# Attention and output projection one head later, V projected in a unit's third step, one DMA transpose for both halves of a head's result

## The reference

```python
q, k, v = h @ dequant(q_w), h @ dequant(k_w), h @ dequant(v_w)   # 32, 8, 8 heads of 128
q, k = rope(q), rope(k)
k, v = repeat(k, 4), repeat(v, 4)
scores = einsum('bhqd,bhkd->bhqk', q, k) * 128 ** -0.5 + mask    # causal
attn = softmax(scores)
out = einsum('bhqk,bhkd->bhqd', attn, v)
y = out.reshape(b, s, 4096) @ dequant(o_w)                       # 4096 -> 512
```

## Time and profile before

| what | us |
|---|---|
| median of 3 runs (lowest, highest) | 1589.76 (1585.22, 1591.85) |
| the profiled execution: its own time, its span | 1594.79, 1593.0 |
| busy in the span: PE, DVE, ACT, POOL | 1440.8, 1218.2, 936.1, 914.7 |
| granted PE clock, mean | 0.978 |

### The profile page before, as it was taken

One profiled execution on the slowest core, in us unless ns is written; L12 is line 12 of the kernel. 1 busy time (PEld: TensorE's weight loads), 2 busy tenths in 40 slices (PEclk: granted clock), 3 DMA queues, 4 the chain that ended last, 5 costly groups with the idle time before them and its releaser, 6 DMA issues.

```text
span 1593.0 us, 41176 instructions
## 1 busy us (share of the span) xinstructions
PE 1440.8 (90%) x11104; PEld 858.2 (54%) x11104; DVE 1218.2 (76%) x2884; ACT 936.1 (59%) x2198; POOL 914.7 (57%) x642
## 2 busy tenths in 40 slices
PE   5787898999999999998999999988999986999998
PEld 3454555556555555655555555555555553544543
DVE  7766688788878787877887888777878887776744
ACT  2555666667666666676666666666666763422411
POOL 3566676667766776776677667766676763110100
PEclk9999899999999999999999999999999998999999
DMA  7479888878787778877888788778778866010100
GB/s 241 95 154 179 165 161 158 151 153 159 153 154 153 158 156 145 159 158 152 150 161 165 151 150 160 156 150 152 147 161 156 153 140 122 14 53 21 34 27 27
DMA packets 526713, 217.17 MB, mean 136 GB/s; under 512 B 483041, under 2 KB 484801, under 8 KB 526529
## 3 DMA queue, kind: packets, MB, share of 16 engines
q1 hardware_dynamic: 524064, 210.54, 66.1%
q0 software_dynamic: 2464, 4.23, 1.6%
HBM read 55.32 MB, written 4.19 MB: 37 GB/s over the span
## 4 chain that ended last, share of the span: by engine, by line
PE 51%; issue 11%; DMA 10%; SPq 8%; DVE 7%; POOL 6%; ACT 5%; DVEq 1%; POOLq 0%; ACTq 0%
PE ps_p L792 4%; PE ps_p L790 4%; POOL p_lo L508 4%; PE ps_p L791 4%; PE ps_s L1023 4%; PE ps_s L1024 4%; PE ps_p L814 3%; DMA ot_lo<-o_lo 3%; PE ps_p L815 3%; PE ps_o L843 3%; PE ps_o L845 2%; PE ps_o L844 2%; PE ps_p L1037 2%; PE ps_p L1038 2%; PE ps_s L827 2%
## 5 line engine op out<-in xcount | busy, mean ns | idle before, releaser
L508 POOL TENSOR_TENSOR p_lo<-prob,p_hi 128x1280 f16<-128x1280 f32 x128 | 344.3, 2689 | 182.3 <-ACT p_hi L636 170.5
L1114 DVE SCALAR_TENSOR_TENSOR y<-ps_p,wo_scale,y 128x512 f32<-128x512 f32 x512 | 381.3, 746 | 73.9 <-PE ps_p L815 52.2
L627 ACT ACTIVATE prob<-prob,exp_bias 128x512 f32<-128x512 f32 (+3 forms) x512 | 283.3, 554 | 143.5 <-DVE exp_bias L1136 140.6
L843 PE MATMUL ps_o<-v_hi,ffn_w 128*128 128x128 f16 x1280 | 229.3, 223 | 95.2 <-issue 51.2
L1127 DVE CUSTOM_DVE_ANT_0 prob<-ps_s,mask 128x512 f32<-128x512 f32 (+3 forms) x512 | 238.0, 483 | 78.8 <-PE ps_s L829 78.5
L790 PE MATMUL ps_p<-x_hi,w_hi 128*128 128x512 f16 x640 | 244.9, 383 | 2.3 <-DVE x_lo L1082 1.4
L791 PE MATMUL ps_p<-x_lo,w_hi 128*128 128x512 f16 x640 | 244.7, 382 | 0.0
L792 PE MATMUL ps_p<-x_hi,w_lo 128*128 128x512 f16 x640 | 244.6, 382 | 0.0
L644 ACT ACTIVATE o_f<-ps_o,inv_sum 128x128 f32<-128x128 f32 x512 | 145.9, 368 | 150.4 <-PE ps_o L845 150.4
L845 PE MATMUL ps_o<-v_hi,ffn_w 128*128 128x128 f16 x1280 | 230.1, 224 | 0.0
L844 PE MATMUL ps_o<-v_lo,ffn_w 128*128 128x128 f16 x1280 | 229.7, 224 | 0.0
(11 more groups left out here) (100 smaller groups left out, 2929.1 us busy)
## 6 DMA issues: line engine op xcount, KB each, us to landing
swap<-other SPq DMA_DIRECT2D x320, 128.0 KB, 3.1
w_code<-w_codes SPq DMA_DIRECT2D x36, 384.0 KB, 3.7
w_scale<-w_scales SPq DMA_DIRECT2D x36, 384.0 KB, 5.0
o_code<-o_codes SPq DMA_DIRECT2D x35, 256.0 KB, 3.0
swap<-x SPq DMA_DIRECT2D x16, 256.0 KB, 2.9
out<-z SPq DMA_DIRECT2D x16, 256.0 KB, 2.0
ffn_w<-x SPq DMA_DIRECT2D x3, 1024.0 KB, 9.7
ffn_w<-p_hi SPq DMA_TRANSPOSE x128, 3.7
```

Of the source, the lines that this page charges most:

```text
L508: pool.tensor_tensor(p_lo[:, :], prob[:, hp, :], p_hi[:, :], ALU.subtract).then_inc(p_lod, 1)
L627: act.activation(prob[:, hp, a:a + w], prob[:, hp, a:a + w], ACT.Exp, bias=exp_bias[:, hp, i:i + 1], scale=-1.0, accum_out=exp_sum[:, hp, ...
L843: pe.matmul(o, ph, vh, start=(i == ORDER[0] and j == 0), stop=False)
L1114: dve.scalar_tensor_tensor(tile, ps_p[:, bank, :], scale, tile, ALU.mult, ALU.add).then_inc(o_add, 1)
```

## The change

Three things at once, in the same tables and loops.

1. In step n PE does `attend(n - 2)` instead of `attend(n - 1)`, and the output tiles are those of head n - 3 instead of n - 2. ScalarE's `o_norm`, GpSimd's `o_low` and SyncE's `turn_o` follow with n - 2. The softmax sums' inverses get four buffers. Unit 0 has attention from step 2 and output from step 3 on; the tail has two heads of attention and three of output, where it had one and two.
2. `FULL` puts V in step 2, behind Q2, and START puts it between Q2 and Q3.
3. o_hi and o_lo lie side by side in o_parts, and one DMA transpose of 1024 columns turns both, once o_lo is done; before, there were two of 512, the first issued when o_hi was done.

```diff
-FULL = (("K", "V"), ("Q0", "Q1"), ("Q2",), ("Q3",))
+FULL = (("K",), ("Q0", "Q1"), ("Q2", "V"), ("Q3",))
-START = ("K", "V", "Q0", "Q1", "Q2", "Q3")
+START = ("K", "Q0", "Q1", "Q2", "V", "Q3")
...
-    return HG * KT * U - 2 * KT
+    return HG * KT * U - 3 * KT
...
+        o_parts = sb("o_parts", [P, 2, S], F16, att)
+        o_hi, o_lo = o_parts[:, 0, :], o_parts[:, 1, :]
+        ot = sb("ot", [P, 2, 2 * TT, P], F16, att)
-        inv_sum = sb("inv_sum", [P, 2, TT], F32, att)
+        inv_sum = sb("inv_sum", [P, HG, TT], F32, att)
...
                 after(sp, o_ps, (n - 1) * KT)
-                sp.wait_ge(oq_hid, n + 1)
-                sp.dma_start_transpose(ot_hi[:, hp, :, :], o_hi[:, :]).then_inc(ot_hi_in, 16)
                 sp.wait_ge(oq_lod, n + 1)
-                sp.dma_start_transpose(ot_lo[:, hp, :, :], o_lo[:, :]).then_inc(ot_lo_in, 16)
+                sp.dma_start_transpose(ot[:, hp, :, :], flat(o_parts[:, :, :])).then_inc(ot_in, 16)
...
                     turn_p_lo(n, h % 2)
-                    if not (first and h == 0):
-                        turn_o(n - 1, (h - 1) % 2)
+                    if not (first and h < 2):
+                        turn_o(n - 2, h % 2)
...
                     p_low(n, h % 2)
-                        o_low(n - 1)
+                        o_low(n - 2)
...
-                        o_norm(n - 1, (h - 1) % 2)
+                        o_norm(n - 2, (h - 2) % HG)
...
                     if nt == 0:
-                        pe.wait_ge(ot_hi_in, 16 * (n - 1))
-                        pe.wait_ge(ot_lo_in, 16 * (n - 1))
-                    if h < 2:
-                        output(U - 1, HG - 2 + h, h, nt, bank_of(r, e))
+                        pe.wait_ge(ot_in, 16 * (n - 2))
+                    if h < 3:
+                        output(U - 1, h + 1, (h + 1) % 2, nt, bank_of(r, e))
...
-                        attend(n - 1, r, (h - 1) % 2, pieces_before(U - 1) + START.index("V") + 1)
+                        attend(n - 2, r, h % 2, pieces_before(U - 1) + START.index("V") + 1)
...
-            attend(UNITS * HG - 1, (UNITS - 1) % 2, 1, 0)
+            attend(UNITS * HG - 2, (UNITS - 1) % 2, 0, 0)
...
+                last_output(1, nt, nt)
+            attend(UNITS * HG - 1, (UNITS - 1) % 2, 1, 0)
...
+            for nt in range(KT):
+                pe.wait_ge(o_add, outs - 2 * KT + nt + 1)
+                last_output(3, nt, (nt + 2) % RING)
```

More of the change, by code:

```diff
@@ L510, in o_low @@
             def o_low(n):
-                after(pool, ot_lo_in, 16 * n)
+                after(pool, ot_in, 16 * n)
                 pool.sem_inc(pool_passed)
@@ L515, in o_low @@
                 pool.sem_inc(pool_passed)
-                pool.tensor_tensor(o_lo[:, :], o_f[:, :], o_hi[:, :], ALU.subtract).then_inc(oq_lod, 1)
+                pool.tensor_tensor(o_lo, o_f[:, :], o_hi, ALU.subtract).then_inc(oq_lod, 1)
             def start_rope(piece):
@@ L644, in o_norm @@
                     act.activation(o_f[:, i * P:(i + 1) * P], ps_o[:, i * P:(i + 1) * P], ACT.Copy,
-                                   scale=inv_sum[:, hp, i:i + 1]).then_inc(oq_norm, 1)
-                after(act, ot_hi_in, 16 * n)
+                                   scale=inv_sum[:, h, i:i + 1]).then_inc(oq_norm, 1)
+                after(act, ot_in, 16 * n)
                 act.wait_ge(oq_norm, (n + 1) * TT)
-                act.activation(o_hi[:, :], o_f[:, :], ACT.Copy).then_inc(oq_hid, 1)
+                act.activation(o_hi, o_f[:, :], ACT.Copy).then_inc(oq_hid, 1)
             def rows_out(t, bank):
@@ L673, in _ @@
             o_centre(0)
+            v_high(0, 0, START.index("V") % 2, START.index("V") + 1)
             rope_high(0, 0, "Q1")
@@ L813, in output @@
                 w = flat(by_half(wo)[:, bass.ds((U >> 2) & 1, 1), h, nt * P:(nt + 1) * P])
-                pe.matmul(ps_p[:, bank, :], w, flat(ot_hi[:, hp, :, :]), start=True, stop=False)
-                pe.matmul(ps_p[:, bank, :], w, flat(ot_lo[:, hp, :, :]), start=False, stop=True).then_inc(o_ps, 1)
+                pe.matmul(ps_p[:, bank, :], w, flat(ot[:, hp, 0:TT, :]), start=True, stop=False)
+                pe.matmul(ps_p[:, bank, :], w, flat(ot[:, hp, TT:2 * TT, :]), start=False, stop=True).then_inc(o_ps, 1)
             def scores(n, U, upar, h, g):
@@ L883, in unit @@
                 names = sequence(slots)
-                idle = place(slots, 2, "O0") if first else 0
+                idle = place(slots, 3, "O0") if first else 0
                 def bank_free(e):
@@ L913, in out_tile @@
                 def out_tile(n, h, nt):
-                    if first and h < 2:
+                    if first and h < 3:
                         return
@@ L1230, in add_last @@
             def add_last(h, nt, bank):
-                add_output(UNITS - 1, NB - 1, h, nt, bank, outs_before(UNITS) + (h - HG + 2) * KT + nt)
+                add_output(UNITS - 1, NB - 1, h, nt, bank, outs_before(UNITS) + (h - 1) * KT + nt)
             def unit(U, b, slots, last=False, first=False):
@@ L1238, in out_tile @@
                     before = outs_before(U) + h * KT + nt
-                    if h > 1:
-                        add_output(U, b, h - 2, nt, bank, before)
+                    if h > 2:
+                        add_output(U, b, 0, nt, bank, before)
                     elif not first:
-                        add_output(U - 1, (b - 1) % NB, HG - 2 + h, nt, bank, before)
+                        add_output(U - 1, (b - 1) % NB, h + 1, nt, bank, before)
                 for h in range(HG):
@@ L1295, in _ @@
             xn_low(TT - 1, ps_p[:, 1, :])
-            for nt in range(KT):
-                add_last(HG - 1, nt, (nt + 2) % RING)
+            for h in (2, 3):
+                for nt in range(KT):
+                    add_last(h, nt, (nt + 2) % RING)
             dve.wait_ge(sc_cv, 4)
```

48 lines of the change are left out of this document (23 added, 25 removed).

## The result

The changed kernel takes 1573.74 us (median of 4 runs, 1573.24 to 1575.74) against 1590.8 for the kernel before: ratio 0.9889, 95% interval 0.984 to 0.9938. It is 1.1% faster, by 17 us where the forecast said 81, and lies above the range of 1486 to 1556. The profiled executions' spans are 1572.4 and 1593.0 us.

What follows compares the result with a forecast made beforehand. TensorE, 36.1 us a unit of its own work, bounds the kernel once its gaps go: 67.3 + 3 + 8.8 + 1.9 = 81.0 us off 1594.8 gives 1513.8, on the median's scale 1509 us; 8 in 10: 1486 to 1556.

Steps and rivals of the forecast that it cites:

- (e): VectorE in the repeated units: its own chain is 34.3 us a unit against PE's 36.1, so it fits by 1.8.
- (c): V moved from the K step to the Q2 step: PE's steps keep the same sum, effect 0.
- (a): Attention, normalisation, output one head later: 67.3 us of attention gaps go; SyncE's later p transposes cost 0, at most 24 us.
- (d): Waits ahead of the output's first matmul: 3 us gained, 14.6 of 17.6 left standing; bounds 17.6 gained, 34 lost.
- R1: Rival: half the attention gain returns as waits for o, 34 us of the 67.3, so 1543 us; chance 0.24.
- (b): One o transpose instead of two: lands in 3.2 us, 0.6 earlier than ot_lo did; SyncE's saved issue counted as nothing.
- (f): Start, units 0 and 1: four attention gaps, 8.8 us with tails, go; the 11.45 us wait at the feed-forward weights' load stays.
- (g): End, last unit and the added attention and output after it: set at 0, between 10 us gained and 8 lost.
- the forecast of the unit: Sign of success in the repeated stretch: a unit, four heads of one batch, takes 36.6 to 36.9 us.

Runs made afterwards that it cites:

- e8: Changed kernel with w_low alone moved ahead of the last output tile of step 3: 1532.91 us, ratio 0.962 to the kernel before.
- e7: Kernel before with only the single 1024-column DMA transpose for o added: 1575.57 us, ratio 0.988.
- e4: Changed kernel with o_hi and o_lo turned by two DMA transposes again: 1615.19 us, ratio 1.015 to the kernel before.
- e9: e8 with ScalarE's v_high also put ahead of p_high in step 2: 1527.12 us, ratio 0.960 to the kernel before.
- e12: e9 with GpSimd's load of down_w held until the last o transpose has landed: 1523.08 us, ratio 0.957 to the kernel before.
- e10: Changed kernel with w_low moved as in e8, V back in step 0, down_w load held until the last o transpose landed: 1542.28 us, ratio 0.970.

## Why the prediction was wrong
**The step that failed is (e)**, "its own chain is 34.3 us a unit against PE's 36.1. It fits, by 1.8 us". The stretch holds 1060.8 / 38.24 = 27.7 units, and VectorE now waits for TensorE 15.1 us in it, so its chain is (1060.8 - 15.1) / 27.7 = 37.7 us a unit, longer than TensorE's 36.1. Of the 3.4 us more, w_lo has 1.4 (2.74 - 1.29), dequant 1.2 (2.66 - 1.48), the wait for v_hi 1.05 (29.1 / 27.7), exp_bias 0.35; that is somewhat more than the whole, so other entries are shorter. I took lengths that were partly waits for another engine as fixed, and they depend on how the two engines stand to each other, which the change moves. e8 shows what it cost: with w_lo at 0.95 us 41 of the 65 us by which the forecast missed are back. The trace of before held the warning: w_lo's 939/942/3394. (e) goes by sums alone, and the rule of the shared ports (the Trainium skill, SBUF — State Buffer, SBUF: two separate sides), which this trace bears out, speaks against carrying such a sum over.

**(c)**, "V moved ... the same sum ... 0", failed with it: the matmuls do have the same sum, but w_lo came to lie on p_lo. It was 8.6 us lost over the units where w_lo stays in its place, 17.6 gained where it does not.

**(a)** was right of the attention: the rows show no wait of TensorE for p in the stretch, and the 11.0 left are waits for VectorE. SyncE waited for the same step's attention 14.2 us in 13 places, where 24 was the bound (the 675.91 quoted there stands in the earlier trace rows, not in the earlier trace rows). **(d)** let 14.6 us of waits for o stand. Reckoned in the same way, there are 38.3 + 63 x 0.17 = 49.0 (the 63 are 26 for the transpose, 21 for y, and 16 in two smaller rows). The sum closes: (1060.8 - 49.0 - 11.0 - 6 x 0.17) / 27.7 = 36.1 us a unit is again TensorE's own work, so this term was right. R1's price, half of 67.3 or 34 us, is what came back at the output (49.0 - 14.6 = 34.4), and another 12.0 us at the attention, where TensorE waits for VectorE. R1's reason (VectorE's lag in step 3 carried on) was the right one; its time, 1543 us, was still 31 us short, since it had neither these 12.0 us nor what the start and the end lost.

**(b)** forecast 3.2 us to landing; the least is 3.0, the median 3.7. The part as a whole, for which the sum has no more than (d)'s 3 us, was worth 19 us alone (e7) and 41 in the changed kernel (e4): a term as large as w_lo's, mis-sized the other way. By the median it lands at 709.12 + 3.7 = 712.8, no sooner than the 712.9 of before, so what it gave is probably SyncE's freed place in the queue, for which "I count nothing"; that is argued, since no run has the one without the other. That it hid a part of what (e) cost was luck.

**(f)** The four attention gaps, 8.1 us, did go, but others came: 4.1 us ahead of the output at 112.6 and 3.4 ahead of the scores at 89.8, where TensorE waits for q_lo. The stall at the feed-forward weights' load stayed, as (f) said, and moved from the attention (11.5 us) to the output (12.0): with it 16.3 us are idle there in 61.5 to 163.9, where before it was 0.2. The start gained 2.8 us of 8.8. Which part of that is owed to what wasn't tried.

**(g)** The end, bounded at 8 lost, lost 10.2. The down_w load beside the last transpose is about 6 us of it, if it costs here what it costs in e9 (81.2 to 74.9 in e12; 3.8 between e8 and e10, which differ in V's place too). The rest fits the third head's output behind the last step, of which (g) spoke, and TensorE's clock: in 1290 to 1312 us the granted clock was 0.77 on the mean, some of it at the lower of its two levels (1.2 GHz), after waits of 3.0 and 2.9 us ahead of the output, and there matmuls of 512 columns show 0.63 us that show 0.38 elsewhere. The end of the kernel before had such stretches too (0.84 in 1300 to 1348), so how much of the difference is the clock stays open.

With w_low moved the unit is 36.96 us, and with v_high too (e9) 36.64, where the forecast was 36.6 to 36.9: the forecast of the unit named what the order of the work allows, and VectorE's standing still and its wait for v_hi were what lay between.

## What to carry to other kernels
Before an engine is called "off the path, with slack", look at the spread of its instructions' lengths, not only at the mean: two lengths for one shape say that the instruction waits inside, and the slack changes as soon as anything shifts. In an in-order queue (here SyncE's) price every entry that stands ahead of a critical transfer, its waits too; here taking one entry away gained 19 us by itself, and a whole step of room by itself lost 15. And when an edit gives less than it should, shift the instruction that got longer before undoing the edit.

## What was new of the hardware
A VectorE product with two inputs in SBUF on 8 columns took 2.43 us on the mean beside a GpSimd operation of 2.6, nearly as long as one of 768 columns (2.74). It works both ways: w_lo first, p_lo 3.36 us; p_lo first, w_lo 3.30. The held one of 768 columns ended 0.81 us after GpSimd's operation each time. An operation with one SBUF input was held too when it had two columns (0.17 us alone, 0.68 on the mean), and never when it had one (0.15). A DMA transpose of 1024 columns landed in 3.0 us at the least and 3.7 in the median, where one of 512 takes 2.4 and the next is issued 1.34 us later. Beside a load of 1280 KB it took 8.2 us.
